# Two experts of a top-2 MoE layer: the weight split of each expert moved into the work ahead of it

## The reference

```python
top_vals, top_idx = top_k(x @ Wr + br, 2)         # 8 experts, N = 8192 tokens
w = softmax(top_vals)
# each expert takes its cap = 1280 heaviest tokens (N / 8 * 1.25)
xe = x[tok]
h1 = gelu(einsum('ech,ehf->ecf', xe, W1) + b1, approximate=False)   # 256 -> 1024
y  = einsum('ecf,efh->ech', h1, W2) + b2                            # 1024 -> 256
out.at[tok].add(y * gate)
```

## Time and profile before

| | |
|---|---|
| median of 3 runs | 1386.81 us (1386.51 to 1387.3) |
| the profiled execution's own time | 1389.0 us |
| its span in the profile | 1387.2 us |
| PE busy | 1163.1 us (84%) |
| DVE busy | 995.6 us (72%) |
| ACT busy | 754.9 us (54%) |
| POOL busy | 971.6 us (70%) |
| routing list ready (IDX written) | 1154.6 us |
| expert blocks | 1168 to 1303 us |
| last norm | 1309 to 1387 us |

### The profile page before, as it was taken

The page is one execution under the profiler, slowest core; times in us unless marked ns, Lnnn a source line. Parts: engine busy times, 40 slices in busy tenths (PEclk is TensorE's granted clock), DMA queues, the critical chain, the costliest instruction groups (busy, mean ns, idle before and its releaser), DMA issues. The chain is left out here.

```text
span 1387.2 us, 23869 instructions
## 1 busy us (share of the span) xinstructions
PE 1163.1 (84%) x5973; PEld 783.3 (56%) x5974; DVE 995.6 (72%) x2205; ACT 754.9 (54%) x1482; POOL 971.6 (70%) x1081
## 2 busy tenths in 40 slices
PE   7899999999999999999999999999931164979500
PEld 5556566665656666565666656565431163979500
DVE  3888687777767777776777778676457884777596
ACT  4565666666576666657666665665413233444144
POOL 3386978878697887869788786978743066545268
PEclk9999999999999999999999999999965555999855
DMA  4000101011010101101010100001032013232474
GB/s 149 16 18 16 58 6 62 16 47 46 15 53 8 62 16 46 46 15 53 9 62 16 46 32 17 32 17 46 31 129 24 18 43 88 43 95 43 87 253 166
DMA packets 68477, 70.89 MB, mean 51 GB/s; under 512 B 12912, under 2 KB 64032, under 8 KB 68272
## 3 DMA queue, kind: packets, MB, share of 16 engines
q1 hardware_dynamic: 46800, 47.18, 10.7%
q10 hardware_dynamic: 16896, 16.78, 3.6%
q0 software_dynamic: 4704, 6.11, 2.9%
HBM read 40.35 MB, written 29.45 MB: 50 GB/s over the span
## 5 line engine op out<-in xcount | busy, mean ns | idle before, releaser
L559 ACT ACTIVATE PF<-PS 128x512 f32<-128x512 f32 x512 | 298.3, 595 | 256.8 <-PE PS L929 247.6
L821 DVE TENSOR_REDUCE NMAX<-PS 128x1 f32<-128x512 f32 x512 | 342.4, 682 | 88.0 <-PE PS L938 84.5
L472 POOL TENSOR_TENSOR SF<-SF,PF 128x512 f32<-128x512 f32 x252 | 322.0, 1300 | 14.7 <-ACT PF L559 14.5
L1010 PE MATMUL PS<-PF,V 128*64 128x512 f32 x1024 | 248.0, 605 | 0.0
L928 PE MATMUL PS<-Q,K 128*128 128x512 f32 x512 | 222.3, 434 | 2.8 <-ACT PF L559 2.8
L938 PE MATMUL PS<-K,Q 128*128 128x512 f32 x512 | 205.5, 403 | 10.6 <-DVE NMAX L821 10.2
L929 PE MATMUL PS<-Q,K 128*128 128x512 f32 x512 | 201.4, 393 | 0.0
L578 ACT ACTIVATE Q<-PS 64x512 fp32r<-64x512 f32 x256 | 151.5, 592 | 48.3 <-PE PS L94 43.3
L469 POOL TENSOR_TENSOR SF<-PF 128x512 f32<-128x512 f32 x126 | 162.0, 1301 | 19.6 <-ACT PF L559 19.6
L500 POOL TENSOR_TENSOR XL<-XF,XH 128x512 fp32r<-128x512 f32 x63 | 82.6, 1312 | 128.5 <-ACT XH L633 128.4
L928 PEld LDWEIGHTS PS<-Q,K 128*128 128x128 f32 x512 | 96.5, 188 | 120.5 <-ACT PF L559 54.6
(11 more groups left out here) (327 smaller groups left out, 2519.7 us busy)
## 6 DMA issues: line engine op xcount, KB each, us to landing
X<-in_L_attn_x SPq DMA_DIRECT2D x16, 512.0 KB, 3.4
MODB<-mod_rows SPq DMA_DIRECT2D x16, 512.0 KB, 3.7
h_rows<-H ACTq DMA_DIRECT2D x16, 512.0 KB, 3.0
acc_rows<-H ACTq DMA_DIRECT2D x16, 512.0 KB, 4.1
out_x<-X SPq DMA_DIRECT2D x16, 512.0 KB, 2.9
A<-acc_rows SPq DMA_DIRECT2D x15, 512.0 KB, 8.8
W1F<-in_L_ffn_W SPq DMA_DIRECT2D x3, 1024.0 KB, 4.9
W2F<-in_L_ffn_W SPq DMA_DIRECT2D x3, 1024.0 KB
```

Of the source, the lines that this page charges most:

```text
L472: s_sum.done(pool.tensor_tensor(total, total, tile, ALU.add))
L559: s_exp.done(act.activation(PF[:, u % 8, :], st_bank(u), ACT.Exp))
L821: s_mred.done(dve.tensor_reduce(NMAX[:, p % 2, r:r + 1], mx_bank(u), AX.X, ALU.max, negate=True))
L1010: last = pe.matmul(num_bank(p)[odd * R:(odd + 1) * R, :], V1[:, vp, c, :], PF[:, k % 8, :], start=(c == 0), stop=(c == TC - 1))
```

## The change

1. The split tiles `W1H`, `W1L`, `W2H`, `W2L` become tiles that live through routing and experts; some tiles of the routing now share memory, and the last norm's `A` lies over the weights.
2. The split of `W1` is done in two halves of 512 inner columns.
3. First expert: ACT makes `W1H` (two halves) and `W2H` at the end of its routing program. DVE makes the first half of `W1L` there, behind the one-hot tiles and ahead of the wait for the list.
4. Next expert: in the last block of an expert, ACT makes the next `W1H` behind the last Gelu and, when PE has finished the block's second layer, a dummy Copy and `W2H`; DVE makes the first half of `W1L` ahead of `YS`. The same instructions run in the last block of the last expert, with the third pair of loads.
5. At an expert's start DVE takes the gates, splits the tokens, makes the second half of `W1L`, then `W2L`. PE waits for the second half of `W1L` ahead of group 4.
6. POOL waits for the list (`s_idx`) behind the register loads from the table, no longer ahead of them.
7. SP waits for the first block's rows ahead of its loop of next loads; the load of `W1F` waits for both halves of `W1L`. In the last norm SP also waits for the last `W2H` ahead of loading `A`.

```diff
@@ route, ACT, at its end
         m["s_h2out"].wait(act, NB - 1, 1)
+        high_weights_1(act, m, 0)
+        high_weights_2(act, m, 0)
@@ route, DVE, behind the one-hot loop
+        low_weights_1(dve, m, 0, 0)
         dve.wait_ge(s_list, 1)
@@ new functions
+def high_weights_1(act, m, a):
+    m["s_w1"].wait(act, a, 0)
+    for j in range(2):
+        cols = half_of_inner(j)
+        m["xs"]["w1h"].done(act.activation(m["W1H"][:, :, cols], m["W1F"][:, :, cols], ACT.Copy))
+def high_weights_2(act, m, a):
+    m["s_w2"].wait(act, a, 0)
+    m["xs"]["w2h"].done(act.activation(m["W2H"][:, :, :], m["W2F"][:, :, :], ACT.Copy))
+def low_weights_1(dve, m, a, j):
+    cols = half_of_inner(j)
+    m["xs"]["w1h"].wait(dve, a, j)
+    m["xs"]["w1l"].done(dve.tensor_tensor(m["W1L"][:, :, cols], m["W1F"][:, :, cols], m["W1H"][:, :, cols].bitcast(F32), ALU.subtract))
@@ experts, SP
         nact = actives(sp)
+        sp.wait_ge(s_gx.sem, 16 * BT)
         with sp.Fori(0, nact) as a:
...
-            s_w1l.wait(sp, a, 0)
+            s_w1l.wait(sp, a, 1)
@@ experts, POOL
-        pool.wait_ge(m["s_idx"], 1)
-        each(pool, None, block, block)
+        def first(e, a, g):
+            pool.wait_ge(m["s_idx"], 1)
+        each(pool, first, block, block)
@@ experts, ACT
-        def expert(e, a, g):
-            act.activation(DUMMY[:, 0:1], IDENT[:, 0:1], ACT.Copy)
-            s_w1.wait(act, a, 0)
-            s_m1.wait(act, g, -1)
-            s_w1h.done(act.activation(W1H[:, :, :], W1F[:, :, :], ACT.Copy))
-            s_w2.wait(act, a, 0)
-            s_m2.wait(act, g, -1)
-            s_w2h.done(act.activation(W2H[:, :, :], W2F[:, :, :], ACT.Copy))
...
-        each(act, expert, block, block)
...
+        def last(e, a, g, k):
+            block(e, a, g, k)
+            high_weights_1(act, m, a + 1)
+            s_m2.wait(act, g, FC - 1)
+            act.activation(DUMMY[:, 0:1], IDENT[:, 0:1], ACT.Copy)
+            high_weights_2(act, m, a + 1)
+        each(act, None, block, last)
@@ experts, DVE
         def expert(e, a, g):
-            s_w1h.wait(dve, a, 0)
-            s_w1l.done(dve.tensor_tensor(W1L[:, :, :], W1F[:, :, :], W1H[:, :, :].bitcast(F32), ALU.subtract))
             next_gates(e, g)
             split_tokens(g)
+            low_weights_1(dve, m, a, 1)
             s_w2h.wait(dve, a, 0)
...
             if more:
                 split_tokens(g + 1)
+            else:
+                low_weights_1(dve, m, a + 1, 0)
@@ experts, PE
             for f in range(LEAD, FC):
+                if f == FC // 2:
+                    s_w1l.wait(pe, a, 1)
                 mm1(g, f)
@@ last_norm, SP
+        nact = sp.value_load(m["INFO"][0:1, 3 * E:3 * E + 1], min_val=1, max_val=E)
+        m["xs"]["w2h"].wait(sp, nact, 0)
         m["xs"]["sc"].wait(sp, total + 2, BLK // P - 1)
```

More of the change, by code:

```diff
@@ L130, in build_program, with sbk @@
             attention(nc, ap, m, sem, sba)
[L131 to L134, removed]
         m["GBG"], m["s_gbg"] = sb("GBG", [P, NB, D]), sem("tgbg")
+        m["INFO"], m["GATEp"] = sb("INFO", [1, 3 * E + 2], I32), sb("GATEp", [P, 7])
         m["s_w1"], m["s_w2"], m["s_b"] = Stream(sem("fw1"), 1, 16, 0), Stream(sem("fw2"), 1, 16, 0), sem("fb")
-        expert_tiles(m, sem, sb)
         with nc.Block() as block:
[L139 to L142, removed]
+            with ExitStack() as kept:
+                def sbk(name, shape, dt=F32):
+                    return sb(name, shape, dt, kept)
+                m["IDX"] = sbk("IDX", [P, E * CAP // P], U32)
+                m["W1F"], m["W2F"] = sbk("W1F", [P, KC, F]), sbk("W2F", [P, F // P, D])
+                m["B1R"], m["B2"] = sbk("B1R", [E * F // P, P]), sbk("B2", [P, E, D])
+                expert_tiles(m, sem, sbk)
+                with ExitStack() as tiles:
+                    route(nc, ap, m, sem, lambda name, shape, dt=F32: sb(name, shape, dt, tiles), block)
+                with ExitStack() as tiles:
+                    experts(nc, ap, m, sem, lambda name, shape, dt=F32: sb(name, shape, dt, tiles), block)
             with ExitStack() as tiles:
@@ L1058, in route @@
     HI, LO, LOW, GT, EQT, SEL, SCAN, DST, ZT = (sb(x, [P, T]) for x in ("HI", "LO", "LOW", "GT", "EQT", "SEL", "SCAN", "DST", "ZT"))
-    BITS, JUNK = sb("BITS", [P, 2, T], U32), [sb(f"JUNK{j}", [P, T]) for j in range(BASE - 1)]
     SAME, LOWER, ONES, DIFF = m["SAME"], sb("LOWER", [P, P]), sb("ONES", [P, P]), sb("DIFFr", [P, P], I32)
@@ L1076, in route @@
     TOK1, IOT = sb("TOK1", [P, 2, NCH]), sb("IOT", [P, P])
+    with ExitStack() as digits:
+        BITS = digits.enter_context(nc.sbuf_tensor("BITS", [P, 2, T], U32))
+        JUNK = [digits.enter_context(nc.sbuf_tensor(f"JUNK{j}", [P, T], F32)) for j in range(BASE - 1)]
     OB, OE, OA = sb("OB", [P, 2, RING, P], F32R), sb("OE", [P, 2, RING, SLOTC]), sb("OA", [P, 2, RING, SLOTC], F32R)
@@ L1416, in expert_tiles @@
     x = {}
-    for k in ("w1h", "w2h", "w1l", "w2l"):
-        x[k] = S("f" + k, 1)
+    for k, per in (("w1h", 2), ("w2h", 1), ("w1l", 2), ("w2l", 1)):
+        x[k] = S("f" + k, per)
+    for k, shape in (("W1H", [P, KC, F]), ("W1L", [P, KC, F]), ("W2H", [P, FC, D]), ("W2L", [P, FC, D])):
+        m[k] = sb(k, shape, F32R)
     x["gx"], x["sc"], x["tok"] = S("fgx", 1, 16 * BT, 0), S("fsc", BT, 16, 0), S("ftok", 4)
@@ L1427, in expert_tiles, with half_of_inner @@
     m["NOUGHT"] = sb("NOUGHT", [P, BT], U32)
-    m["YS"], m["GATEp"] = sb("YS", [P, BT, D]), sb("GATEp", [P, 7])
+    m["YS"] = sb("YS", [P, BT, D])
+def half_of_inner(j):
+    return slice(j * (F // 2), (j + 1) * (F // 2))
+def high_weights_1(act, m, a):
[10 more added lines that the diff above has]
+    m["xs"]["w1l"].done(dve.tensor_tensor(m["W1L"][:, :, cols], m["W1F"][:, :, cols], m["W1H"][:, :, cols].bitcast(F32), ALU.subtract))
 def scatter(pool, m):
@@ L1461, in experts @@
     W1F, W2F, B1R, B2 = (m[x] for x in ("W1F", "W2F", "B1R", "B2"))
-    W1H, W1L = sb("W1H", [P, KC, F], F32R), sb("W1L", [P, KC, F], F32R)
-    W2H, W2L = sb("W2H", [P, FC, D], F32R), sb("W2L", [P, FC, D], F32R)
+    W1H, W1L, W2H, W2L = (m[x] for x in ("W1H", "W1L", "W2H", "W2L"))
     B1, DUMMY = sb("B1", [P, E * FC]), m["DUMMY"]
```

## The result

| | changed | before |
|---|---|---|
| median, this comparison (8 runs each) | 1382.8 us (1381.68 to 1387.05) | 1387.66 us |
| ratio, 95% | 0.9968 (0.9954 to 0.9982) | |
| the profiled execution, its span | 1385.23, 1383.4 us | 1389.0, 1387.2 us |
| measured again (11 and 21 runs) | 1384.33 us | 1387.81 us |
| ratio, 95% | 0.9972 (0.9963 to 0.9981) | |

The change makes the kernel faster by 0.3%, 3.5 to 4.9 us by the medians, where 6.65 were forecast (1380.2 us). The two profiled executions differ by 3.77 us.

The account below looks back on a forecast made before the run. PE bounds steady blocks; outside them it waits for rows and weight splits. Gains of 5.65 (first expert) and 1.15 (second), less 0.15 at the end, give 6.65 us: 1380.2 us on the median, range 1377.2 to 1384.2.

Parts of the forecast that it names:

- first transposes: First expert's first block: rows at 1160.75 against 1167.99, 7.2 us earlier.
- second block's rows: First expert: rows land about 1172.8 against 1178.45, gaining 5.65 us (3.5 to 5.95).
- clock behind the stall: Rival: PE's longer stall at the first expert's second block lowers its clock, costing 2.5 us, so 1382.7; chance 0.15.
- second expert's start and rows: Second expert: PE's start 2.35 us earlier, next rows 1.15; 1.15 us gained, up to 2.35.
- last block: Second expert's last block: half a `W1H` and half a `W1L` ahead of `YS` cost 0.15 us.
- The work in the routing: Ahead of the list: ACT's copies and DVE's half `W1L` cost nothing, with 1 us of cover left on DVE.
- The rival of free descriptors: POOL's operations get in between DVE's, both stalls for rows nearly vanish: 8.8 us gained, 1378.0; chance 0.17.
- table load in the last block: Rival: ACT's copies behind Gelu reload a table, 1.28 us later in both last blocks, so 1382.7; chance 0.05.
- the old case: Late bound for the second block's rows: landing 4.5 us behind their descriptors, at 1174.9.
- the slower rival: Second block's rows land no sooner than 1178.45, PE stands 9 us, the clock costs 2.5 us: 1391.8; chance 0.05.
- one chain of three gains: First expert's first rows: POOL's start 2.8 us earlier, descriptors 1.8 us shorter, landing 2.6 us shorter.

Follow-up runs that it names:

- the second trace: The changed kernel measured again with no edit, beside the others on one chip: 1384.33 us, 0.9972 of the kernel before.
- the table read alone: The kernel before, with only POOL's wait for the list moved behind its register loads: 1383.26 us, 0.9974.
- late loads: The changed kernel, with SP issuing the next expert's loads only after the rows of each expert's second block have landed: 1379.64 us, 0.9938.
- with the tiles moved: The changed kernel with SP's next loads behind the second block's rows and the split weight tiles at the addresses of the kernel before: 1379.36 us, 0.9934.
- without prepared weights: The kernel before, with POOL's wait behind its register loads and SP's next loads behind the second block's rows: 1380.63 us, 0.9945.
- the changed kernel with 192 bytes ahead: The changed kernel with 192 bytes of padding ahead of the four split weight tiles and 320 behind them: 1384.32 us, a single run.

## Why the prediction was right, and where its steps were off

Measured by the same events as above, behind the list:

| step | forecast | measured |
|---|---|---|
| first transposes | 7.2 | 7.0 |
| second block's rows | 5.65 left | 4.32 left |
| clock behind the stall | 0 (a rival, -2.5) | -1.6 |
| steady blocks, both experts | 0 | -0.6, -0.7 |
| second expert's start and rows | +1.15 | +2.6 |
| last block | -0.15 | -0.4 |
| sum | 6.65 | 3.57 |

**Right.** The direction and the range held (1382.8 in 1377.2 to 1384.2), though with some luck: measured again, the median is 1384.33, just outside, and the gains of 4.9 and 3.5 us are 0.73 and 0.52 of the 6.65 forecast. In the table two misses that I had not priced against each other, +1.45 at the second expert and -1.3 in the steady blocks, nearly cancel. What did come as forecast is the first step: it came out to 0.2 us, with POOL's first operation 2.9 us sooner (2.8 forecast), descriptors of 0.97 us (1.0 to 1.1), landing 2.55 us behind their end instead of 4.75 (2.1). The work in the routing was covered. POOL's small operations were held by half `W1L` and `W2L`, as I had it, but one after the other: the index copy came through at 1164.48, between the two, so that the descriptors ended 15.20 us behind the list instead of 15.83. The rival of free descriptors fell for the first expert. There was no table load in the last block.

**The step that failed** is the landing of the second block's rows. I had computed that 2 MB of loads "are 5.0 us from 1166.5, the rows (0.27 MB) 0.65 more", 2.4 us behind the descriptors, and kept the 4.5 of the old case as the far end. Measured: 4.36 us, and 3.58 in the second trace. The order was right, the weights first and the rows last. The size was wrong, and in the first trace the transposes started 1.3 us later behind the list than forecast. Half of that is the rate, by an estimate: 418 GB/s was moved in a stretch with packets of `W1F` alone, 4 KB each, but from 1167 to 1171, mostly with the 1 KB packets of `W2F`, it was 378 GB/s; 2.37 MB take 6.3 us at that rate and 5.65 at 418. The rest lies in the end, 1171 to 1173, where rows and last weights together moved only 296 GB/s, and in the 0.5 us until PE had the rows; what slows the end is open. The old case, with one load beside, was the nearest row, and I passed it over for a calculation. For the slower rival I called 4.5 us "the most seen", though the first block's 4.75 stood in my own rows; the runs went up to 5.49. The Trainium skill (DMA: Bandwidth & Descriptors, "Queues, rings and completion order") says that an engine takes turns between queues packet by packet. I had taken from it that rows need not wait for weights. The trace doesn't agree with that: for 3 us only weights moved. By the page the turn is a group of up to 64 descriptors, so it may be as long as that; no run here shows the groups. With the loads behind them the rows land in 1.87 us, so here they paid 2.5 us for what went ahead.

**The clock** followed from it. With a stall of 4.30 us the rival of the lower clock happened: in the block behind it the gain fell from 4.32 to 2.70. I had set it against the forecast as an alternative with 0.15; it hung on the same uncertain landing, so a later landing should have carried the lower clock with it. Its cost was 1.6 us here and 2.8 in the second trace, for 2.5 forecast. That the rival's time, 1382.7, is almost the measured one is chance, since the other steps moved as well.

**The second expert** was under-priced. I took the descriptors to end behind `W2L` (1.15 us) and kept 2.35 for the case that they slip in between the two DVE instructions. They did: they started 0.15 us before `W2L` and took 1.10 us. Their end came 4.9 us sooner than before behind the list (83.84 against 88.74), and the rows landed 4.72 us behind it, so the stall for rows stayed (0.96 us).

**Unforeseen:** the slower steady blocks, 1.3 us over both experts in this trace. The last block's -0.4 holds its share of this, so that I can't check the 0.15 charged there; the row on `YS` with 0.26 us of waiting for PE says that the half `W1L` ahead of it was hidden.

**What the change is made of.** I had treated the 5.65 us of the first expert as one chain of three gains. The runs show that the table read alone gets 7 us at the first transposes, since POOL is then ahead of DVE's `W1L` in time. The prepared weights remove a neighbour that was no longer one. In the first expert PE starts 0.2 us earlier by them and gets the second block's rows 1.1 us later (0.5 in the second trace); at the second expert its wait falls from 4.04 to 2.32 us, and its second block starts 1.0 us earlier behind the list (88.56 against 89.56); the steady blocks are slower. At the last `YS` nothing is left, 144.47 against 144.28 us. The kernels that beat both have late loads: 1379.64 us, or 1379.36 with the tiles moved as well, 0.5 to 0.8% below the kernel before by the intervals, and 1380.63 without prepared weights. Which of them is best isn't told apart.

## What to carry to other kernels

Ahead of a wait for late data, do what needs no data (register loads, loop headers): here one moved wait was worth as much as the whole change. When a step becomes earlier, ask which transfers it now meets, and let a small gather written behind a large load wait for most of that load, as here, at the rate that the loads reach together, or price it by a row that has such a neighbour. If a stall hangs on that landing, let the lower clock hang on it too, as one case.

## What the hardware did that I had not expected

- A block's rows (two gathers of 128) landed 1.87 to 2.98 us behind their last descriptors where no load had been issued ahead of them. Where one or two had, in the first expert of the kernel before and in seven other traces, it was 3.58 to 5.49 us. With two loads ahead, 822 packets of weights and none of the rows moved in 3 us, though the first gather's descriptors had been written; without loads all 96 packets of the rows had moved 1.6 us behind the last descriptors.
- After stalls of 2.50 and 2.87 us ahead of the second block PE was granted 0.50, for the first of them after 1 us at full clock (late loads with the tiles moved; the changed kernel with 192 bytes ahead), where 2.36, 1.66, 1.19 and 0.95 us were followed by 1.00. All five stalls of 3.75 to 5.83 us were followed by the 1.2 GHz level. So was the 2.32 us at the changed kernel's second expert (0.57 over 4 us), where PE had just done four transposes between two waits.
- While DVE subtracts two tiles of 2048 columns, POOL's operation on one column lasts until DVE is done: 2.15 us in the changed kernel, 0.19 with nothing beside. Descriptors started behind such an instruction end some 0.9 us after it, which made 2.90 us out of about 1. Descriptors that had started 0.15 us ahead of such an instruction were written in 1.10 us beside it, and then the next small operation was held.
- A matmul of 256 columns took 0.120 us in steady blocks (40 us over 334) with one place of the split tiles and 0.118 (40 over 339 or 340) with three others, at full clock and with PE busy throughout.
